# Decays of a state-space scan: the cross-chunk factor from two tables on VectorE, the in-chunk exponents on quarters of the array

## The reference

```
xch = (hs * dt[..., None]).reshape(b, nc, CHUNK, H, P)
A_cum = jnp.cumsum(A_dt, axis=-1)
L = jnp.exp(_segsum(A_dt))                       # within a chunk, l >= s
Y_diag = einsum('bzlhn,bzshn,bhzls,bzshp->bzlhp', Cc, Bc, L, xch)
decay_states = jnp.exp(A_cum[..., -1:] - A_cum)
states = einsum('bzlhn,bhzl,bzlhp->bzhpn', Bc, decay_states, xch)
Y_off = einsum('bzlhn,bzhpn,bhzl->bzlhp', Cc, prev, jnp.exp(A_cum))
Y = (Y_diag + Y_off) + hs * D
```

## Time and profile before

| | us |
|---|---|
| median of 3 runs (lowest, highest) | 1862.39 (1862.04, 1862.73) |
| the profiled execution, whole | 1863.36 |
| its span | 1861.6 |
| mean granted TensorE clock in it | 0.986 of full |

### The profile page before, as it was taken

The page is one execution under the profiler, slowest core; times in us unless marked ns, Lnnn a source line. Parts: engine busy times, 40 slices in busy tenths (PEclk is TensorE's granted clock), DMA queues, the critical chain, the costliest instruction groups (busy, mean ns, idle before and its releaser), DMA issues.

```text
span 1861.6 us, 35838 instructions
## 1 busy us (share of the span) xinstructions
PE 1805.1 (97%) x10520; PEld 1448.8 (78%) x10520; DVE 1256.5 (67%) x2147; ACT 918.5 (49%) x1660; POOL 1006.2 (54%) x812
## 2 busy tenths in 40 slices
PE   5799999999999999999999999999999998999998
PEld 4577887788777877787778777887788776788886
DVE  6588728872887377746884688457754884877776
ACT  4466526652665256635663566346644663222221
POOL 4266645664566446654665366546654657633430
PEclk9899999999999999999999999999999997999999
DMA  2211101110111011101120111001101111111101
GB/s 93 63 53 41 46 3 45 52 52 0 47 53 52 0 47 51 53 0 36 46 64 6 29 53 53 17 29 53 47 23 30 42 35 53 40 52 35 51 17 46
DMA packets 49019, 74.94 MB, mean 40 GB/s; under 512 B 10356, under 2 KB 18676, under 8 KB 48984
## 3 DMA queue, kind: packets, MB, share of 16 engines
q1 hardware_dynamic: 47976, 73.12, 12.9%
q10 hardware_dynamic: 1008, 1.38, 0.2%
HBM read 70.35 MB, written 4.06 MB: 40 GB/s over the span
## 4 chain that ended last, share of the span: by engine, by line
PE 94%; DVE 2%; POOL 1%; issue 1%; ACT 1%; POOLq 0%; DVEq 0%; ACTq 0%
PE proj L758 16%; PE proj L760 16%; PE proj L759 16%; PE y L891 7%; PE y L945 6%; PE y L947 6%; PE y L946 6%; PE y L881 4%; PE trb L858 3%; PE diff L867 3%; PE y L758 2%; PE y L760 2%; PE y L759 2%; PE misc L867 1%; PE misc L931 1%
## 5 line engine op out<-in xcount | busy, mean ns | idle before, releaser
L758 PE MATMUL proj<-xhi,w_hi 128*128 128x512 f32 x1088 | 466.1, 428 | 5.4 <-DVE v L1068 5.4
L760 PE MATMUL proj<-xhi,w_lo 128*128 128x512 f32 x1088 | 426.2, 392 | 0.0
L759 PE MATMUL proj<-xlo,w_hi 128*128 128x512 f32 x1088 | 425.5, 391 | 0.0
L406 POOL TENSOR_TENSOR w_lo<-w_raw,w_hi 128x512 fp32r<-128x512 f32 x144 | 184.1, 1297 | 227.5 <-ACT w_hi L536 227.5
L1068 DVE SCALAR_TENSOR_TENSOR v<-proj,par_sb,v 128x510 f32<-128x510 f32 (+2 forms) x384 | 282.1, 742 | 14.9 <-ACT v L558 11.6
L758 PEld LDWEIGHTS proj<-xhi,w_hi 128*128 128x128 f32 x1088 | 205.0, 188 | 75.5 <-issue 7.9
L462 POOL TENSOR_TENSOR g_lo<-gated,g_hi 128x512 fp32r<-128x512 f32 x128 | 163.8, 1283 | 182.1 <-ACT g_hi L689 182.0
L760 PEld LDWEIGHTS proj<-xhi,w_lo 128*128 128x128 f32 x1088 | 204.8, 188 | 46.5
L759 PEld LDWEIGHTS proj<-xlo,w_hi 128*128 128x128 f32 x1088 | 205.4, 189 | 38.6
L1163 DVE TENSOR_TENSOR M<-diff,cb 128x512 f32<-128x512 f32 x256 | 170.4, 686 | 82.2 <-ACT diff L644 82.2
L945 PE MATMUL y<-wo_hi,g_hi 128*128 128x512 f32 x512 | 202.9, 396 | 4.0 <-POOL g_lo L462 4.0
(11 more groups left out here) (179 smaller groups left out, 3420.1 us busy)
## 6 DMA issues: line engine op xcount, KB each, us to landing
w_raw<-in_win SPq DMA_DIRECT2D x144, 256.0 KB, 2.7
wo_raw<-in_wout SPq DMA_DIRECT2D x64, 256.0 KB, 2.6
M<-in_w SPq DMA_DIRECT2D x14, 512.0 KB, 3.7
cb<-in_w SPq DMA_DIRECT2D x7, 512.0 KB, 3.4
row_l<-rows_l SPq DMA_DIRECT2D x192, 6.0 KB
out<-resid SPq DMA_DIRECT2D x8, 256.0 KB, 2.0
rows_l<-gated SPq DMA_DIRECT2D x9, 128.0 KB, 2.5
resid<-in_x SPq DMA_DIRECT2D x4, 256.0 KB, 4.7
```

What stands on the lines that cost most here:

```text
L406: e.tensor_tensor(w_lo[:, slot, i, :], w_raw[:, i, :], w_hi[:, slot, i, :].bitcast(F32), ALU.subtract).then_inc(split.sem, 1)
L758: e.matmul(o, hi_l, hi_r, start=first, stop=False)
L759: e.matmul(o, hi_l, lo_r, start=False, stop=False)
L760: return e.matmul(o, lo_l, hi_r, start=False, stop=last)
```

## The change

- Kind 1 (chunk 0 to chunk 1) no longer comes from PE and ACT. Two tables are made once: fade_s, exp(sum after s), stays in SBUF for all heads; fade_l, exp(A_cum[l]), is stored to memory as faded, and SP loads two heads of it per tile, spread over all partitions. DVE makes M for it in eight instructions of 128 columns (weigh_past: table * scalar * C.B).
- The other two kinds are four matmuls, each from 15 rows at partitions 0, 32, 64 or 96, so each on its own quarter of the array's rows, into two double banks decay0 and decay1 (z is the chunk). ACT and DVE handle 1024 columns at once (bounded, exponential, weigh_own).
- The rows come by eight small DMAs a tile instead of four.
- y is made in one block of 24 matmuls behind unit 3.
- The transposes go into y's banks, both after unit 0, and wait for y_summed.
- The squares sq have one buffer, and POOL alternates square and sum.
- At the start B and C of group 0 are projected first, then hs and gate of tile 0.

```
-                def exponents(q):
-                    kind, head = q // 2, q % 2
-                    pe.wait_ge(mdone.sem, mdone.at(g, j, q - 2))
-                    at_l = row_r[:, par_, head, :].rearrange("p (b z l) -> p z b l", b=B, z=2)[:, int(kind > 0), :, :]
-                    e.matmul(dbank[q % 3][:, :].rearrange("p (b l) -> p b l", b=B),
-                             row_l[:, par_, head, kind * P:(kind + 1) * P], at_l,
-                             start=True, stop=True).then_inc(dready.sem, 1)
+                def exponents():
+                    pe.wait_ge(mdone.sem, mdone.at(g, j, 0))
+                    pe.wait_ge(s_rowq[par_], (TPG * 64) * g + 64 * j + (128 - 64 * par_))
+                    pe.wait_ge(cbd.sem, cbd.at(g, 0, 0))
+                    for z in range(2):
+                        for head in range(2):
+                            first = 32 * (2 * z + head)
+                            mm = e.matmul(decay[z][:, head * HALF:(head + 1) * HALF],
+                                          row_l[first:first + PARTS + PARTS * B, par_, :],
+                                          row_r[first:first + PARTS + PARTS * B, par_, :], start=True, stop=True)
+                        mm.then_inc(dready.sem, 1)
...
+                def y():
+                    pe.wait_ge(mdone.sem, mdone.at(g, j, PAST + OWN))
+                    pe.wait_ge(xdts.sem, xdts.at(g, j, 2))
+                    for b in range(B):
+                        cols = slice(b * P, (b + 1) * P)
+                        for z, part, slot in ((0, 0, 0), (1, 0, 4), (1, 1, 2)):
+                            for head in range(2):
...
-                turn(0)
...
-                exponents(0)
-                exponents(1)
+                exponents()
                 if nxt:
                     unit(0)
+                turn(0)
                 turn(1)
-                exponents(2)
-                exponents(3)
                 if nxt:
                     unit(1)
-                y_first()
-                exponents(4)
-                exponents(5)
-                if nxt:
                     unit(2)
                     unit(3)
-                y_second()
+                y()
...
+                bounded(0)
+                bounded(1)
+                exponential(0)
                 w = tile_weights(TPG * g + j + 1)
                 if nxt:
                     tap3(0, w, ready.at(g, j, 1), silu.at(g, j, -1))
-                decay(2)
-                decay(3)
+                exponential(1)
...
+                def weigh_past(head):
+                    dve.wait_ge(s_fade[head], (16 * TPG) * g + 16 * j + 16)
+                    dve.wait_ge(cbd.sem, cbd.at(g, 0, 0))
+                    dve.wait_ge(yready.sem, yready.at(g, j, 0))
+                    for b in range(B):
+                        cols = slice(b * P, (b + 1) * P)
+                        ins = e.scalar_tensor_tensor(
+                            M[:, 4 + head, cols], fade_l[:, head, cols],
+                            fade_s[:, bass.ds(2 * t + head, 1), b:b + 1].rearrange("p a b -> p (a b)"),
+                            cb[:, 1, cols], ALU.mult, ALU.mult)
+                    ins.then_inc(mdone.sem, 1)
...
                 w = tile_weights(t + 1)
+                weigh_past(0)
+                weigh_past(1)
+                weigh_own(0)
                 times_dt(0)
-                weigh(0)
-                weigh(1)
                 times_dt(1)
                 if nxt:
-                    conv_rest(0, w, tap.at(g, j, 1), convs.at(g, j, 0),
-                              (lambda: weigh(2), lambda: weigh(3)))
+                    conv_rest(0, w, tap.at(g, j, 1), convs.at(g, j, 0), (lambda: weigh_own(1),))
...
             def step(g, j, par_, nxt, nxt2):
                 sp.wait_ge(wolo.sem, wolo.at(g, j, 0))
                 sp.dma_start(wo_raw[:, :], wout[TPG * g + j, :, :]).then_inc(woraw.sem, 16)
                 if nxt:
-                    sp.wait_ge(dready.sem, dready.at(g, j, 1))
+                    sp.wait_ge(dready.sem, dready.at(g, j, 0))
                     load_rows(TPG * g + j + 1, 1 - par_)
+                    sp.wait_ge(mdone.sem, mdone.at(g, j, PAST))
+                    load_fade(TPG * g + j + 1)
```

More of the change, by code:

```diff
@@ L285, in load_pair @@
                     sp.dma_start(w_raw[:, i, :], win[n, i, :, :]).then_inc(s_raw[i], 16)
[L287 to L288 removed]
+            for k, n in enumerate((1, 0, 2)):
+                load_pair(n, 2 * k if k else None)
             def load_rows(t, par_):
[L291 to L295, removed]
@@ new lines, in _ @@
+            sp.wait_ge(s_fade_l, 2)
+            sp.dma_start(faded, faded_sb).then_inc(s_faded, 16)
+            for k in range(PARTS):
+                sp.wait_ge(s_part[k], 1)
+                for z in range(2):
+                    sp.dma_start(rows[:, z, k, :, :],
+                                 parts[:, k, :].rearrange("h (b z l) -> h z b l", b=B, z=2)[:, z, :, :])\
+                        .then_inc(s_rows, 16)
+            sp.wait_ge(s_faded, 16)
+            load_fade(0)
+            sp.wait_ge(s_rows, 32 * PARTS)
@@ L411, in split_pair @@
                     split_piece(slot, i, parts)
[L413 to L423, removed]
+            split_pair(1, 0)
+            split_pair(0, 2)
+            pool.wait_ge(s_part[0], 1)
+            e.tensor_tensor(rem, acum, parts[:, 0, :], ALU.subtract).then_inc(s_rest[0], 1)
+            pool.wait_ge(s_rest[0], 1)
+            pool.wait_ge(s_part[1], 1)
+            e.tensor_tensor(parts[:, 2, :], rem, parts[:, 1, :], ALU.subtract).then_inc(s_part[2], 1)
             split_pair(1, 4)
@@ L879, in y_first @@
                     for b in range(B):
-                        for head in range(2):
-                            mm = e.matmul(ybank[b // 2][head * HD:(head + 1) * HD, (b % 2) * S:(b % 2) * S + P],
-                                          xdt[:, 2 * b, head * HD:(head + 1) * HD],
-                                          M[:, SLOT[head], b * P:(b + 1) * P], start=True, stop=True)
-                    mm.then_inc(yready.sem, 1)
-                def y_second():
-                    pe.wait_ge(mdone.sem, mdone.at(g, j, 6))
-                    for b in range(B):
-                        for part in range(2):
+                        cols = slice(b * P, (b + 1) * P)
@@ L1115, in _ @@
             link(e.scalar_tensor_tensor(dtq, dtv, 0.0, dtq, ALU.max, ALU.add))
+            for h in range(2):
+                hs_silu(bc[:, 0, :], h, h + 1)
             dt_flat = dt[:, :, :].rearrange("p t f -> p (t f)")
@@ L1121, in _ @@
                 .then_inc(s_dta, 1)
-            conv_rest(1, w, 2, 2)
-            hs_silu(hs[:, 0, :], 0, 1)
-            hs_silu(hs[:, 0, :], 1, 2)
-            gate_silu(gate[:, 0, :], 0, 3)
-            gate_silu(gate[:, 0, :], 1, 4)
-            bc_tile(0, 0, 2, 4, 4, bc_banks[0][0])
-            bc_tile(0, 1, 2, 4, 4, bc_banks[0][1])
+            w = bc_weights(0, 1)
+            conv_rest(0, w, 3, 4, banks=bc_banks[0][1])
+            conv_rest(1, w, 4, 6, banks=bc_banks[0][1])
+            for h in range(2):
+                hs_silu(bc[:, 1, :], h, h + 3)
+            w = tile_weights(0)
+            conv_rest(0, w, 5, 8, banks=diff)
+            conv_rest(1, w, 6, 10, banks=diff)
+            for h in range(2):
+                hs_silu(hs[:, 0, :], h, h + 5)
             def cbs_kept(ncb):
@@ L1142, in _ @@
             cbs_kept(1)
+            gate_silu(gate[:, 0, :], 0, 7)
+            gate_silu(gate[:, 0, :], 1, 8)
+            dve.wait_ge(s_fade_s, 1)
             def step(g, j, par_, nxt, nxt2):
```

283 lines of the change are left out of this document (133 added, 150 removed).

## The result

The changed kernel takes 2284.3 us (median of 4 runs, 2283.4 to 2285.4) against 1862.2 us before (4 runs beside them, 1861.7 to 1862.7): a ratio of 1.227, 95% interval 1.225 to 1.229. It is 22.7% slower. The forecast was 1941 us, range 1906 to 1992: the direction was right, the time lies far outside.

A forecast was written before the change was run, and what follows sets the result against it. PE, busy 97%, bounded the kernel; after the change it would wait for DVE, 1.5 us more in 63 tiles: 1863.4 + 94 - 14 - 1 = 1942, the median run 1 lower, about 1941 us, range 1906 to 1992.

The forecast's parts named there:

- ACT's three passes: On ACT, early in each tile: three 1024-column passes before the first product, ready 3.38 us after the exponents begin.
- the chain: On DVE, after ACT's passes: products, times-dt and conv steps sum to 5.52 us, so PE waits 2.35 before unit 2.
- the start: At the kernel's start: B and C first and shorter POOL memsets give -14 us, bounds -8 and -18.
- PE's list: PE's own work in a tile: exponents 0.35, units 10.95, transposes 0.9, y 2.95, together 15.15 us.
- Being nearest in width, I take 0.32: DVE's eight table products early in each tile: 0.32 us each, just hidden by ACT; bounds 0.25 and 0.53 each.
- the forecast tile: One tile, from exponents to the next exponents: 17.8 to 17.85 us against the old 16.35, 1.5 more.
- Clock: Rival, chance 0.22: PE's clock falls after the stall, 2.4 us in every third tile, +50, about 1990 us.
- PE's sum decides: Rival, chance 0.12 including a chain at least 1.2 us shorter: PE's work sets the tile, 15.15; kernel about 1771 us.

The follow-up runs named there:

- experiment 6: Experiment 4's kernel with VectorE's order alone changed: both convolutions ahead of the second own product and both times-dt; factor of s left out; 1832.0 us, ratio 0.984.
- experiment 1: Changed kernel with the second tensor of the eight table products read from a bank of y in PSUM, values meaningless; 1967.6 us, ratio 1.057.
- experiment 3: Changed kernel with GpSimd's squares and sums, four instructions a tile, made memsets of the same tiles; 2059.3 us, ratio 1.106.
- experiment 4: Changed kernel with one product of 1024 columns in place of the eight table products, factor of s left out; 1962.5 us (one run).
- experiment 8: Experiment 6's kernel made the whole computation: the factor of s comes back as eight ScalarE operations a tile; 1834.5 us, ratio 0.986.

## Why the prediction was wrong

By its own steps:
- *ACT's three passes, the chain, the start.* Right. Where GpSimd was idle the tile was 18.02 for 17.8 and the wait 2.38 for 2.35; the 5.52 us chain was found again in the long tile (341.68 to unit 2 at 347.47 is 5.79, of which 0.15 was said to be PE's start); the start gave 15 for 14.
- *PE's list, 15.15.* Too short by 0.3 to 0.5: at full clock PE's own work is 15.64 in the first tile above (18.02 less 2.38) and 15.47 in experiment 6. The exponents (0.33), transposes (0.79) and y (2.77) were not dearer than said, but the units take 2.88 to 2.99 from start to start, not 2.75. This hardly shows beside the wait, but it is one reason why the rival that lived on this sum, 1771 us, was never reached.
- *"Being nearest in width, I take 0.32 ... At 0.53 it ends at 5.04 and adds 1.6 us."* **This step failed.** The eight took 2.2 us where nothing disturbed them (2.56 said) and 7.3 elsewhere. The products ended 8.0 us after E instead of 3.4, so 4.6 us came on top of the forecast tile. Neither bound could hold that: both rows, and the earlier trace rows, are of instructions with one tensor from SBUF, or ran without GpSimd beside them. What GpSimd does at that moment was missing from the argument; the trace of before had two rows on it, which stand below this list, and the prediction looked at GpSimd only as a producer.
- The rule was there to be read. The Trainium skill, SBUF — State Buffer, "Who interferes with whom", says that a VectorE instruction with two SBUF inputs and a GpSimd instruction that reads SBUF exclude each other for the whole length of an instruction. Experiments 1 and 3 agree, one with each condition: 342 against 1123 ns when one input moves to PSUM, and 2059.3 against 2059.7 us when the GpSimd instructions only write.
- *Clock.* Priced 2.4 us in every third tile, with 0.22. In the changed kernel it fell behind every wait near 7 us, for about 1.7 us (0.86 over the second tile above). 17.8 + 4.6 + 1.7 is 24.1, and the median tile is 24.0. In experiments 1 and 4, whose waits are near the forecast ones (2.1 us), it fell in a little over a third of the tiles for 1.45: some 30 us, and 1941 + 30 is near their 1968 and 1962. The rival was right in kind and in frequency for the wait that it assumed, and 1 us too dear per tile.
- *PE's sum decides, 1771.* The chain could be shortened, but the sum was 15.5, not 15.15, and 0.6 us of wait stayed: 1832 (without the factor of s; 1834.5 with it).

The first of the two rows is the tile of the earlier trace rows: in the 7.3 us from E (515.08) on, GpSimd gates, squares and sums.

```profile
515.34 2.56 POOL L438 TENSOR_TENSOR gated<-hs,gate 128x512 f32 x2
517.84 2.06 POOL L447 TENSOR_TENSOR sq<-gated 128x512 f32 x2
519.83 2.56 POOL L452 TENSOR_TENSOR sqacc<-sqacc,sq 128x512 f32<-128x512 f32 x2
```

The second is the wait itself. At the start of the kernel before, the same pair of VectorE instructions, M and v both in SBUF, stands once beside GpSimd (65.32 to 69.01) and once with GpSimd idle until 76.14:

```profile
65.32 3.69 POOL L419 TENSOR_TENSOR gated<-gated 128x1024 f32<-128x1024 f32 x2 [37.46 <-ACT gated L609]
```
```profile
66.33 3.23 DVE L1082 SCALAR_TENSOR_TENSOR M<-M,v 128x512 f32<-128x512 f32 x2 [5.89 <-ACT M L569]
...
74.81 1.47 DVE L1082 SCALAR_TENSOR_TENSOR M<-M,v 128x512 f32<-128x512 f32 x2
```

The two instructions last 1.67 and 1.64 us the first time, 0.68 and 0.69 the second. Each of the slow ones ends about 0.55 us behind the end of a GpSimd instruction.

In terms of the whole: the two-input products 317 us (experiment 1), the chain's order about 130 (experiment 6 against 4), and the change with neither some 30 us faster than before (experiment 6; experiment 8, the whole computation, 26). Not separated by a run of its own: how much of the 317 is wait and how much the clock that fell after the longer wait; by the tiles (24.0 against 18.3) about 4.6 to 1.1.

## What to carry to other kernels

Before putting many small VectorE instructions with two SBUF tensors beside a busy GpSimd, count them: each can wait for a whole GpSimd instruction that reads SBUF, whatever its own size. Read one operand from PSUM, make one wide instruction of them, or give the scaling to ScalarE. When a cost is bounded from nearest rows, the rows must match in where the operands lie and in what the neighbouring engines do at that time, not only in width. And of two edits on one chain, look at order first: here it was worth 130 us for no change of work (208 with all eight products in place).

## What the runs showed of the hardware

- VectorE's wait for GpSimd isn't shown as a wait: it lengthens the instruction (337 to 1482 ns for one and the same) and hides in "busy". A series pays it again and again: eight products and six GpSimd instructions took 7.3 us together.
- It goes both ways: beside the one long product of experiment 6 GpSimd's two gating instructions took 3.5 us together, and 2.6 in the changed kernel.
- ScalarE on the same tiles in SBUF is not slowed by GpSimd: of the 512 scalings of experiment 8, 421 lie wholly beside a GpSimd instruction and 20 beside none, and both last 0.39 us in the median.
- Waits of PE of 2.1 us (experiments 1 and 4) were followed by a lower clock in a little over a third of the tiles; after the 55 waits near 7 us it fell each time.
- Four matmuls on a quarter of the rows each, 512 columns, start to start with what follows: 0.33 us for the four (315.63 to 315.96 in the changed kernel).
